# A one-core transformer block: vector fills in pieces, second norm formed transposed

## What is computed

```python
xn = _layernorm(x)                       # no weight, no bias
x = x + attn(xn)  + ffn(xn)

def ffn(x):                              # x is xn here
    n1 = _layernorm(x, ln1_w, ln1_b)     # a second norm of an already normed row
    rw = _gating(n1, smha_sim, gates)    # 8 weights per row, two at least
    q = einsum('btc,ech,bte->bth', n1, q_proj, rw)      # k, v alike
    attn = softmax(causal(q k^T / sqrt(128))) v
    hs = x + einsum('bth,ehc,bte->btc', attn, o_proj, rw)
    n2 = _layernorm(hs, ln2_w, ln2_b)
    rw2 = _gating(n2, moe_sim, moe_gates)
    inter = gelu(einsum('btc,eci->btei', n2, w1))
    return hs + einsum('btei,eic,bte->btc', inter, w2, rw2)
```

## Time and profile before

| | us |
|---|---|
| median of three runs | 1325.96 |
| lowest, highest | 1323.41, 1326.18 |
| profiled execution | 1324.63 |
| its span, first to last instruction | 1322.7 |
| mean granted clock of PE | 0.958 of full speed |

### The profile page before, as it was taken

One profiled execution on the slowest core, in us unless ns is written; L12 is line 12 of the kernel. 1 busy time (PEld: TensorE's weight loads), 2 busy tenths in 40 slices (PEclk: granted clock), 3 DMA queues, 4 the chain that ended last, 5 costly groups with the idle time before them and its releaser, 6 DMA issues.

```text
span 1322.7 us, 33146 instructions
## 1 busy us (share of the span) xinstructions
PE 1203.3 (91%) x10652; PEld 917.5 (69%) x10652; DVE 1034.0 (78%) x3697; ACT 718.8 (54%) x1292; POOL 222.4 (17%) x342
## 2 busy tenths in 40 slices
PE   2599989898989898989898979898999989999998
PEld 1377767676767676767676757676787767777776
DVE  8899969696969696969696969696997577777664
ACT  4166646464646464646464646464656865555532
POOL 4112111111111111111111211121231100000000
PEclk9899989897989897989898989898999999999999
DMA  4533322322222222222222222222233144444453
GB/s 106 147 107 107 91 87 81 83 81 82 80 83 82 82 82 82 80 84 82 82 81 82 82 81 82 82 82 82 83 93 91 38 149 161 161 161 161 162 195 140
DMA packets 103172, 133.50 MB, mean 101 GB/s; under 512 B 13576, under 2 KB 82424, under 8 KB 94864
## 3 DMA queue, kind: packets, MB, share of 16 engines
q1 hardware_dynamic: 100548, 130.72, 31.9%
q10 hardware_dynamic: 2508, 1.58, 0.5%
HBM read 109.12 MB, written 21.54 MB: 99 GB/s over the span
## 4 chain that ended last, share of the span: by engine, by line
PE 52%; DVE 27%; issue 17%; DVEq 2%; ACT 1%; DMA 1%; ACTq 1%; POOL 0%; SPq 0%; POOLq 0%
PE ps L1890 8%; PE ps L1876 8%; PE ps L1613 5%; PE ps L1623 4%; PE ps L1659 4%; PE ps L1614 4%; DVE mx L1210 3%; PE ps L1590 3%; PE ps L1486 2%; DVE rots L1129 2%; PE ps L1539 1%; PE ps L1549 1%; PE ps L1573 1%; DVE rots L1126 1%; DVE rots L1135 1%
## 5 line engine op out<-in xcount | busy, mean ns | idle before, releaser
L1210 DVE TENSOR_REDUCE mx<-ps 128x4 f32<-128x1024 f32 (+1 forms) x192 | 234.9, 1223 | 80.0 <-PE ps L1549 33.1
L779 ACT ACTIVATE pr<-ps 128x1024 f32<-128x1024 f32 x192 | 196.6, 1024 | 170.3 <-PE ps L1573 104.4
L636 POOL TENSOR_TENSOR n1s<-rep,n1T 128x256 f32<-128x256 f32 x256 | 177.3, 730 | 323.8 <-DVE mpart L1224 307.1
L785 ACT ACTIVATE ps<-trn 128x1024 f32<-128x1024 bf16 x191 | 196.5, 1029 | 5.1
L1613 PE MATMUL ps<-n1s,wqk 128*128 128x256 f32 x512 | 180.0, 436 | 0.0
L1890 PEld LDWEIGHTS ps<-w2s,ats 128*128 128x128 f32 x1024 | 131.4, 191 | 52.7 <-issue 43.9
L1614 PE MATMUL ps<-n1s,wqk 128*128 128x256 f32 x512 | 166.3, 409 | 0.0
L979 ACT ACTIVATE n1s<-ps 128x512 f32<-128x512 f32 x128 | 76.6, 598 | 121.0 <-PE ps L1876 119.9
L1890 PE MATMUL ps<-w2s,ats 128*128 128x128 f32 x1024 | 136.0, 276 | 2.4 <-DVE ats L1414 2.4
L1623 PE MATMUL ps<-wv,n1s 128*128 128x128 f32 x1024 | 133.1, 278 | 0.0
L1876 PE MATMUL ps<-rep,w1s 128*128 128x512 f32 x256 | 130.7, 594 | 0.0
(11 more groups left out here) (229 smaller groups left out, 2074.9 us busy)
## 6 DMA issues: line engine op xcount, KB each, us to landing
rep<-scr_rw SPq DMA_DIRECT2D x32, 1024.0 KB, 5.7
stk<-scr_rw SPq DMA_DIRECT2D x16, 1024.0 KB, 8.6
scr_parts<-parts SPq DMA_DIRECT2D x64, 192.0 KB, 5.8
stk<-scr_parts SPq DMA_DIRECT2D x248, 48.0 KB
rots<-scr_rw SPq DMA_DIRECT2D x8, 1024.0 KB, 4.7
wqk<-scr_rw SPq DMA_DIRECT2D x8, 1024.0 KB, 9.1
stk<-scr_parts SPq DMA_DIRECT2D x248, 32.0 KB
xt<-in_x SPq DMA_DIRECT2D x32, 128.0 KB, 2.2
```

Of the source, the lines that this page charges most:

```text
L636: pool.tensor_tensor(n1s[:, e], rep[:, par, e], n1T[:, par], ALU.mult).then_inc(n1s_done, 1)
L779: act.activation(pr[:, Q, :, i], ps[:, S2[0]:S2[0] + NF], ACT.Exp).then_inc(exp_done, 1)
L785: act.activation(ps[:, S2[0]:S2[0] + NF], seeds[:, kind:kind + 1].broadcast_to((P, NF, 512)), ACT.Copy).then_inc(seed_done, 1)
L1210: dve.tensor_reduce(mx[:, min(i, 1)].rearrange("p (f h) -> p f h", f=NF)[:, :, h:h + n], ps[:, S1[0]:S1[0] + NF].rearrange("p f (h t) -> p ...
```

## The change

Two things are changed.

1. The fills `ones_p` and `mpart` at the head of DVE's program are made in eight pieces each instead of one; the counts that others wait for follow.
2. For blocks 3 to 31 z is no longer made by rows and transposed. PE transposes xn alone, ACT copies 256 columns. GpSimd stores the 256 roots to DRAM by a DMA of its own (`store_roots`), reads them back spread over all partitions (`spread_roots`, between the second and the third `n1s` of the step), and makes z transposed as a product of `xnT` and the spread roots (`second_norm_T`) behind the eighth `n1s`. ACT's `evac_norm_1` waits for that product. Two products of one column (`turn_over`) stand ahead of the copy and of the spread. Blocks 0 to 2 go the old way.

```diff
+NP_FRONT = 3
...
+            def keep(b):
+
+                pool.wait_ge(ln_chain, LN1_LINKS * (b + 1))
+                pool.tensor_tensor(turn_over[:, 0:1], ones_p[:, 0:1], ones_p[:, 0:1], ALU.mult)
+                hv = hs[:, T * b:T * b + T] if isinstance(b, int) else hs[:, bass.ds(b * T, T)]
+                pool.tensor_copy(hv, xn[:]).then_inc(keep_done, 1)
+
+            def store_roots(b):
+
+                pool.dma_start(scr_r2.rearrange("i p -> p i"), rstd[:, 1, 0:T], allow_slow_non_contiguous=True
+                               ).then_inc(r2_stored, 16)
+
+            def spread_roots(b):
+
+                pool.wait_ge(r2_stored, 16 * (b - NP_FRONT + 1))
+                pool.tensor_tensor(turn_over[:, 1:2], ones_p[:, 0:1], ones_p[:, 0:1], ALU.mult)
+                pool.dma_start(rrep[:], scr_r2.rearrange("(o i) p -> o (i p)", o=1).broadcast_to((P, S))
+                               ).then_inc(rrep_in, 16)
+
+            def second_norm_T(b):
+
+                pool.wait_ge(rrep_in, 16 * (b - NP_FRONT + 1))
+                pool.wait_ge(xnT_done, b + 1)
+                pool.wait_ge(n1T_done, b)
+                pool.tensor_tensor(xzT[:, 1], xzT[:, 0], rrep[:], ALU.mult).then_inc(zT_done, 1)
+
             def step(n, u, n_x):
                 if n_x == 3:
-                    second_norm(n + 3)
+                    keep(n + 3)
+                    store_roots(n + 3)
                 if n_x:
-                    scale(n + 1, 1 - u)
+                    scale(n + 1, 1 - u, range(2))
+                if n_x == 3:
+                    spread_roots(n + 3)
+                if n_x:
+                    scale(n + 1, 1 - u, range(2, E))
+                if n_x == 3:
+                    second_norm_T(n + 3)
...
             def evac_norm_1(b, par):
 
-                act.wait_ge(xnT_done, b + 1)
+                if isinstance(b, int) and b < NP_FRONT:
+                    act.wait_ge(xnT_done, b + 1)
+                else:
+                    act.wait_ge(zT_done, b - NP_FRONT + 1)
...
                 dve.wait_ge(ln_out, b + 1)
+                if not isinstance(b, int) or b > NP_FRONT:
+                    dve.wait_ge(zT_done, b - NP_FRONT)
                 c.add(dve.tensor_tensor(rstd[:, 1, 0:T], t[:, 0:T], y[:, T:2 * T], ALU.mult))
...
-            ch.add(dve.memset(ones_p[:], 1.0))
+            for k in range(FILLS_ONES):
+                ch.add(dve.memset(ones_p[:, k * P // FILLS_ONES:(k + 1) * P // FILLS_ONES], 1.0))
...
-            ch.add(dve.memset(mpart[:], 0.0))
+            mparts = mpart[:].rearrange("p i h -> p (i h)")
+            for k in range(FILLS_MAX):
+                ch.add(dve.memset(mparts[:, k * S // FILLS_MAX:(k + 1) * S // FILLS_MAX], 0.0))
...
-                pe.wait_ge(zp_done, b + 1)
-                for k, src in enumerate((xn[:], zt[:])):
+                front = isinstance(b, int) and b < NP_FRONT
+                if front:
+                    pe.wait_ge(zp_done, b + 1)
+                for k, src in enumerate((xn[:], zt[:]) if front else (xn[:],)):
```

More of the change, by code:

```diff
@@ L132, in build @@
     scr_rw2 = nc.dram_tensor("scr_rw2", (4, E, TM, P), F32, kind="Internal").ap()
+    scr_r2 = nc.dram_tensor("scr_r2", (T, P), F32, kind="Internal").ap()
     scr_base = nc.dram_tensor("scr_base", (NB, P, T, D), F32, kind="Internal").ap()
@@ L182, in build @@
         zt = sb("zt", [P, T, D])
+        rrep = sb("rrep", [P, S])
+        turn_over = sb("turn_over", [P, 2])
         bst = sb("bst", [P, 2, TM, 6])
@@ L265, in build @@
         zp_done = sem("zp_done")
+        r2_stored = sem("r2_stored")
+        rrep_in = sem("rrep_in")
+        zT_done = sem("zT_done")
         xnT_done = sem("xnT_done")
@@ L351, in build @@
         N_ROWS = 2 * NF + 2 * NF
-        N_FILL = 7
+        FILLS_ONES, FILLS_MAX = 8, 8
+        N_FILL = 5 + FILLS_ONES + FILLS_MAX
         SIN_READY, N_SET_DVE = N_FILL + 11, N_FILL + 12
@@ L626, in masks, with scale @@
                 c.close()
-            def scale(b, par):
+            def scale(b, par, which=range(E)):
                 pool.wait_ge(rep_in, 16 * (b + 1))
@@ L634, in scale @@
                     pool.wait_ge(max_chain, (MAX_LINKS + 1) * (b + 1))
-                for e in range(E):
+                for e in which:
                     pool.tensor_tensor(n1s[:, e], rep[:, par, e], n1T[:, par], ALU.mult).then_inc(n1s_done, 1)
@@ L724, in evac_norm_x @@
                 act.wait_ge(v_out, b)
-                act.activation(xzT[:], ps[:, banks[0]].rearrange("p (a t) -> p a t", a=2), ACT.Copy).then_inc(xnT_done, 1)
+                if isinstance(b, int) and b < NP_FRONT:
+                    act.activation(xzT[:], ps[:, banks[0]].rearrange("p (a t) -> p a t", a=2), ACT.Copy
+                                   ).then_inc(xnT_done, 1)
+                else:
+                    if not isinstance(b, int) or b > NP_FRONT:
+                        act.wait_ge(zT_done, b - NP_FRONT)
+                    act.activation(xzT[:, 0], ps[:, banks[0], 0:S], ACT.Copy).then_inc(xnT_done, 1)
             def evac_norm_1(b, par):
-                act.wait_ge(xnT_done, b + 1)
+                if isinstance(b, int) and b < NP_FRONT:
+                    act.wait_ge(xnT_done, b + 1)
+                else:
+                    act.wait_ge(zT_done, b - NP_FRONT + 1)
                 if not isinstance(b, int) or b > 1:
@@ L1292, in layer_norm2 @@
                 else:
-                    dve.wait_ge(zp_done, NB)
+                    dve.wait_ge(r2_stored, 16 * (NB - NP_FRONT))
                 bsf, bmf = (v[:].rearrange("p a i k -> p (a i) k") for v in (bst, bmv))
```

## The result

| | before | after |
|---|---|---|
| median, us | 1326.07 (4 runs, 1323.41 to 1329.04) | 1293.38 (4 runs, 1287.05 to 1298.69) |
| profiled execution, us | 1324.63 | 1287.05 |
| mean granted clock of PE | 0.958 | 0.985 |

A forecast was written before the change was run, and what follows sets the result against it. The prediction blamed DVE's instruction fetches at the loop's 12 jumps, 8.6 us each: profiled 1324.6 - 103.3 (fills) + 4.6 (second norm) = 1225.9, with the median 1.3 higher: 1227 us, range 1210 to 1292.

The follow-up runs named there:

- the five placements: The kernel before (1326.07 us), and the kernel before with 6, 8, 14 and 46 more fills: 1355.0, 1217.7, 1216.9 and 1263.3 us.

## What to carry to other kernels
Cost a DMA twice: by who waits for it, and by what else runs until it is done, other queues' transfers first; count its contiguous pieces, not its bytes. When an instruction is put into a row of one engine, see which instruction of the engine that it shares SBUF with now starts inside that row. In a hardware loop, find how the body lies on the instruction packets of each engine before anything else is tuned, and measure every other change on both sides of the edge: here two fills outweigh all else, and a change that adds a few instructions ahead of a loop can gain or lose 10% by that alone.

## What the runs showed of the hardware
- DVE's instructions come in packets of 8 KB, 128 instructions. Four are kept; a jump to a kept one costs nothing (28.4 us per step), a jump to a missing one 2.7 us (with 46 more fills), and where the next edge is one instruction behind it 8 us (with 6). The packets are counted on queue 14; where the edges lie and that four are kept is worked out from the five placements.
- A store to DRAM of 1 KB in 256 pieces of 4 bytes takes 9.9 us (8.3 to 10.8), in 128 pieces of 8 bytes 4.0 to 4.4 (medians of two kernels). Other queues' packets barely move until it is done (0.10 MB in 9 us in place of 0.45). If the pieces are shared out evenly over the 16 engines, it is 16 for each, one after the other at 0.6 us (an estimate from the 9.9 us). The Trainium skill (DMA: Bandwidth & Descriptors, Queues, rings and completion order) says that an engine drains a whole packet of one queue before it turns to another; the trace agrees with the order of events, but no run here shows it directly. Issued from SP it also holds SP's own issues (10.7 us for nine).
- A DVE product with both operands in SBUF can stand through three GpSimd instructions in a row: 2.59 us on average for 0.69 of work, in 22 steps. The Trainium skill (SBUF — State Buffer, SBUF: two separate sides) has the lock held for one whole instruction; by that DVE would have got in at 595.7, and it did at about 597. Where it starts inside the last `n1s`, it is let in ahead of the product (1.17 us). What decides between the two stays open; no run varied it alone.
- In every kernel that makes the store of 4-byte pieces each step, and in no other, an instruction sometimes stands until about the time that the store is done, with no event that the profile names: ACT's `ov` in the changed kernel (7 times, at most 2.8 us), and with the store on SP's queue also DVE's `gs` at L1245 (at most 3.1 us). By what way the store holds it stays open.
